# Two-layer graph network with a 4096 x 4096 adjacency matrix: high parts of split units copied into three matmul banks as well, low parts subtracted from there piece by piece

## What is computed

```python
def _lap_mul(A, x):
    d = 1.0 / jnp.sqrt(jnp.sum(A, axis=-1))
    return d[:, None] * (A @ (d[:, None] * x))
# layer 0, on h = relu(layernorm(x))
z = leaky_relu(_lap_mul(A, h) @ W1 + b1)                 # first product with A
d2 = max(|z_i|^2 + |z_j|^2 - 2 z_i.z_j, 0)               # distances of all pairs
S = exp(-sqrt(d2 + 1e-10) / 2), kept for the 4 best of each row, else 0
x = x + _lap_mul(S + A, h) @ W2 + b2                     # second product with A
# layer 1, on h = relu(layernorm(x))
x = x + h @ W_self.T + (A @ h) @ W_neigh.T + b           # third product with A
```

## Time and profile before

| | us |
|---|---|
| median of 3 runs | 1177.01 |
| lowest, highest run | 1172.3, 1194.65 |
| the profiled execution | 1180.82 |
| its span, first to last instruction | 1178.8 |
| TensorE busy (matmuls) | 929.5 (79%) |
| VectorE busy | 868.9 (74%) |
| GpSimd busy | 680.8 (58%) |
| ScalarE busy | 566.7 (48%) |

### The profile page before, as it was taken

One profiled execution on the slowest core, in us unless ns is written; L12 is line 12 of the kernel. 1 busy time (PEld: TensorE's weight loads), 2 busy tenths in 40 slices (PEclk: granted clock), 3 DMA queues, 4 the chain that ended last, 5 costly groups with the idle time before them and its releaser, 6 DMA issues.

```text
span 1178.8 us, 12596 instructions
## 1 busy us (share of the span) xinstructions
PE 929.5 (79%) x3378; PEld 583.5 (50%) x3378; DVE 868.9 (74%) x960; ACT 566.7 (48%) x1171; POOL 680.8 (58%) x1103
## 2 busy tenths in 40 slices
PE   0146437549559788769999999979989997999997
PEld 0023213224224333346766766435656645788886
DVE  2648558757768999747999998627687648888884
ACT  2454434545422221147777778424334433676763
POOL 9999988878673668104555565667777763000000
PEclk9987679689789888979999999999999998899999
DMA  9999999999999999739766767998989997699992
GB/s 210 293 315 321 330 331 363 341 335 359 361 333 358 339 313 356 296 125 367 260 250 247 256 235 270 395 412 316 349 299 356 371 341 269 248 369 383 376 387 90
DMA packets 98750, 369.10 MB, mean 313 GB/s; under 512 B 21264, under 2 KB 34320, under 8 KB 73872
## 3 DMA queue, kind: packets, MB, share of 16 engines
q1 hardware_dynamic: 51696, 258.43, 56.6%
q0 software_dynamic: 40960, 103.87, 30.7%
q10 hardware_dynamic: 6048, 6.29, 1.6%
HBM read 244.78 MB, written 123.73 MB: 313 GB/s over the span
## 4 chain that ended last, share of the span: by engine, by line
PE 41%; DVE 7%; POOL 5%; issue 4%; DMA 3%; ACT 2%; POOLq 0%; ACTq 0%; DVEq 0%
PE ps L1362 6%; PE ps L1380 5%; PE ps L1381 5%; PE ps L1382 5%; PE ps L1363 5%; PE ps L1364 5%; PE ps L1389 4%; POOL zt_lo L613 3%; PE ps L1359 2%; DVE araw_r L1207 2%; DVE araw L936 1%; DMA araw<-in_adj_dram 1%; DVE out_t L1164 1%; PE ps L1259 1%; PE ps L1271 1%
## 5 line engine op out<-in xcount | busy, mean ns | idle before, releaser
L389 POOL DMA_DIRECT2D araw<-in_adj_dram x704 | 382.7, 552 | 88.5 <-DVE tr L936 48.9
L1207 DVE TENSOR_TENSOR araw_r<-araw,tr_r 128x512 fp32r<-128x512 f32 (+1 forms) x184 | 213.9, 1220 | 63.4 <-ACT tr_r L815 63.3
L815 ACT ACTIVATE tr_r<-araw 128x2048 fp32r<-128x2048 f32 x88 | 166.3, 1910 | 74.4 <-DMA araw<-transposed 29.6
L613 POOL DMA_INDIRECT zt_lo<-neighbour_table,idx_st x128 | 144.2, 1126 | 48.8 <-issue 42.3
L761 ACT ACTIVATE araw<-ps,nsq 128x1024 f32<-128x1024 f32 x128 | 142.6, 1117 | 55.4 <-PE ps L1364 55.4
L1271 PE MATMUL ps<-tr,ys 128*128 128x512 f32 x256 | 130.7, 661 | 35.5 <-DVE ys L943 28.5
L659 ACT ACTIVATE ps<-araw 128x256 f32<-128x256 f32 x304 | 111.6, 367 | 81.9 <-DMA araw<-in_adj_dram 81.4
L936 DVE STREAM_TRANSPOSE tr<-araw 128x2048 f32<-128x2048 f32 x32 | 123.3, 3873 | 30.3 <-DMA araw<-in_adj_dram 26.7
L1389 PE MATMUL ps<-araw,ys 128*128 128x512 f32 x320 | 142.9, 602 | 2.6 <-ACT ys L806 2.6
L1362 PE MATMUL ps<-zt_lo,zs_hi 128*128 128x512 f32 x256 | 108.8, 425 | 0.0
L1066 DVE TENSOR_REDUCE bmax<-araw 128x64 f32<-128x4096 f32 x23 | 101.5, 4411 | 9.4 <-ACT araw L761 7.4
(11 more groups left out here) (164 smaller groups left out, 1460.7 us busy)
## 6 DMA issues: line engine op xcount, KB each, us to landing
araw<-transposed SPq DMA_DIRECT2D x128, 1024.0 KB, 7.1
araw<-in_adj_dram POOLq DMA_DIRECT2D x704, 128.0 KB, 16.2
keys_scratch<-araw SPq DMA_DIRECT2D x96, 512.0 KB, 3.5
transposed<-tr SPq DMA_DIRECT2D x32, 1024.0 KB, 8.6
transposed<-unit_zt_hi SPq DMA_DIRECT2D x8, 1024.0 KB, 9.3
transposed<-unit_zt_lo SPq DMA_DIRECT2D x8, 1024.0 KB, 8.7
transposed<-unit_sq_rows SPq DMA_DIRECT2D x8, 1024.0 KB, 9.5
transposed<-araw SPq DMA_DIRECT2D x8, 1024.0 KB, 5.3
```

Of the source, the lines that this page charges most:

```text
L389: gp.dma_start(araw[R * q:R * q + R, place, U * v:U * v + U], adj_v[q, :, g // 2, g % 2, v, :, c]).then_inc(a_first_in[place], DMA)
L613: gp.indirect_dma_start(out=gath[:, i, u, k, :], out_offset=None, in_=table, in_offset=bass.IndirectOffsetOnAxis(ap=idx_st[:, i, u * TOPK ...
L815: act.activation(ring_hi[:, place % TSLOTS], ring[:, j], ACT.Copy).then_inc(hi_done, 1)
L1207: ins = v.tensor_tensor(ring_lo[:, j, u], ring[:, j, u], ring_hi[:, place % TSLOTS, u].bitcast(F32), ALU.subtract)
```

## The change

In the second product (g2 < 8), ScalarE copies each 512-column piece of the high part once more, from SBUF into one of three PSUM banks (5, 6, 7 in turn), after it has waited for the end of its own 2048-column copy. A copy into a bank waits until VectorE has done the subtraction that read the bank last (`lo_piece`). VectorE's subtraction takes the high part from the bank (`hi_piece`) instead of from SBUF, and raises `lo_piece` per piece. TensorE waits for the count of pieces in the second product, and for `lo_done`, which now counts the third product's units alone, in the third.

```diff
--- before.py
+++ after.py
@@ -189,6 +189,7 @@
         ps_t = ps[:, 3]
         ps_q = ps[:, 4]
         ps_d = ps[:, 5]
+        hi_banks = [ps[:, 5 + i] for i in range(3)]
         junk = [ps[:, 6], ps[:, 7]]
 
         x_in = sem("x_in")
@@ -239,6 +240,8 @@
         h_hi_done = sem("h_hi_done")
         hi_done = sem("hi_done")
         lo_done = sem("lo_done")
+        hi_piece = sem("hi_piece")
+        lo_piece = sem("lo_piece")
         lane_max = sem("lane_max")
         lane_found = sem("lane_found")
         block_maxima = sem("block_maxima")
@@ -813,6 +816,13 @@
                     act.wait_ge(u_used, used_before(g2, j))
                 act.wait_ge(a_in[j], g2 * DMA + DMA)
                 act.activation(ring_hi[:, place % TSLOTS], ring[:, j], ACT.Copy).then_inc(hi_done, 1)
+                if g2 < GROUPS:
+                    act.wait_ge(hi_done, place + 1)
+                    for u in range(U):
+                        n = place * U + u
+                        if n >= len(hi_banks):
+                            act.wait_ge(lo_piece, n - len(hi_banks) + 1)
+                        act.activation(hi_banks[n % len(hi_banks)], ring_hi[:, place % TSLOTS, u].bitcast(F32), ACT.Copy).then_inc(hi_piece, 1)
 
             def evacuate(g, bank, used, turn):
 
@@ -1202,6 +1212,12 @@
             def split_low(g2, j):
 
                 place = split_place(g2, j)
+                if g2 < GROUPS:
+                    for u in range(U):
+                        n = place * U + u
+                        v.wait_ge(hi_piece, n + 1)
+                        v.tensor_tensor(ring_lo[:, j, u], ring[:, j, u], hi_banks[n % len(hi_banks)], ALU.subtract).then_inc(lo_piece, 1)
+                    return
                 v.wait_ge(hi_done, place + 1)
                 for u in range(U) if g2 <= GROUPS else (slice(0, U),):
                     ins = v.tensor_tensor(ring_lo[:, j, u], ring[:, j, u], ring_hi[:, place % TSLOTS, u].bitcast(F32), ALU.subtract)
@@ -1372,9 +1388,9 @@
                 for par in range(2):
                     distances(pair * 2 + par, par)
 
-            def unit(g2, j, bank, hi, lo, place, ready, first, last):
-
-                pe.wait_ge(lo_done, ready)
+            def unit(g2, j, bank, hi, lo, place, split_done, ready, first, last):
+
+                pe.wait_ge(split_done, ready)
                 for i in range(U):
                     t_hi, t_lo = ring_hi[:, place % TSLOTS, i], ring_lo[:, j, i]
                     pe.matmul(acc[bank], hi[:, i], t_lo, start=first and i == 0, stop=False)
@@ -1416,7 +1432,7 @@
                 else:
                     if isinstance(g, int) and g == 1:
                         pe.wait_ge(y_lo_done, j - WHOLE + 1)
-                    unit(g, j, i, y_split[:, j], y_split[:, j - WHOLE], j - WHOLE, g * TSLOTS + (j - GROUPS + 1), False, j == GROUPS - 1)
+                    unit(g, j, i, y_split[:, j], y_split[:, j - WHOLE], j - WHOLE, lo_piece, g * (TSLOTS * U) + (j - GROUPS + 1) * U, False, j == GROUPS - 1)
 
             def group_second(g, i, turn=1):
                 pe.wait_ge(acc_read, g + (2 * GROUPS - 3))
@@ -1437,7 +1453,7 @@
             def group_third(g, i, prev):
                 pe.wait_ge(acc_read, g + (3 * GROUPS - 3))
                 for j in range(GROUPS):
-                    unit(g + GROUPS, j, i, hi_g[:, j], lo_g[:, j], j, g * GROUPS + ((GROUPS - 2) * TSLOTS + j + 1), j == 0, j == GROUPS - 1)
+                    unit(g + GROUPS, j, i, hi_g[:, j], lo_g[:, j], j, lo_done, g * GROUPS + (j + 1), j == 0, j == GROUPS - 1)
                     if prev is not None and j == 0:
                         finish_third(prev)
 
@@ -1470,7 +1486,7 @@
             pe.wait_ge(acc_read, 3 * GROUPS - 3)
             for j in range(GROUPS):
                 pe.wait_ge(kept, j + 2)
-                unit(GROUPS, j, 0, hi_g[:, j], lo_g[:, j], j, (GROUPS - 2) * TSLOTS + j + 1, j == 0, j == GROUPS - 1)
+                unit(GROUPS, j, 0, hi_g[:, j], lo_g[:, j], j, lo_done, j + 1, j == 0, j == GROUPS - 1)
                 if j == 0:
                     finish_second_b(GROUPS - 2)
                     finish_second_a(GROUPS - 1)
```

## The result

The changed kernel took 1206.3 us (median of five runs, 1204.9 to 1230.0), the kernel before 1177.0 (five runs, 1172.3 to 1194.7). The ratio is 1.033 with a 95% interval of 1.026 to 1.040: slower by over 2%, and outside the range of 1173 to 1201. The profiled execution took 1206.0, its span is 1204.1. Medians and ranges in this text take in all runs; a ratio, with its 95% interval in brackets, takes only runs within 1.5% of the kernel's fastest and compares them with such runs of the kernel before in the same set.

The account below looks back on a forecast made before the run. TensorE was taken to bound the kernel; ScalarE's lengthened loop makes it 11.5 us late in the second product, reduced to 5.8 + 1.7 = 7.5 at the third's start: 1177.0 + 7.5 = 1184.5, said as 1185, range 1173 to 1201.

Parts of the forecast that it names:

- Waits: Second product: behind ScalarE's copies stand the evacuation (reading a finished group from its bank), c's input and the next unit.
- c's input: ScalarE's copy feeding TensorE's finishing step c, after the evacuation; with the evacuation counted as 2 x 0.48 us per group.
- the loop's 4.5 us of slack: ScalarE and VectorE's loop took 21.97 us per group against TensorE's 26.44, leaving 4.5 us to spare.
- Prices: Copy 587 ns, 0.50 us each in a run; unit 3.94 us on ScalarE, was 1.80; subtraction 0.61 to 0.69 us.
- Rival 1: Copies cost more, unpipelined 0.65 us, a unit 4.54: 1196 us, or 1202 with slower subtractions; chance 0.18.
- The loop: Second product, ScalarE and VectorE per group: 27.9 us, 1.5 above TensorE's 26.44; evacuation over 12.4 us after the loop's start.
- N(3): ScalarE's start on the next group's split units after normalizing, for group 3: forecast at 842.9 us, was 841.41.
- a(5): TensorE's finishing step a of group 5, waiting for the evacuation: forecast at 939.0 us, was 927.54, so 11.5 late.
- GpSimd freed: Gathers take 1.50 us beside two-SBUF-input subtractions, 1.01 alone; PSUM input may end them microseconds sooner, counted 0 for that alone.
- rival 2: Not slower: copies hide in the loop's slack and freed GpSimd removes a 7.7 us block: 1172 us; chance 0.14.
- The start of the third product: Sums of group 7 begin 5.8 us late, plus 1.7 for VectorE standing still beside GpSimd's adds: 7.5 us.
- Rival 3: VectorE's standing still at the third product's start stays whole: +11.5 us, 1188.5; sign a VectorE piece over 7 us; chance 0.14.

Follow-up runs that it names:

- changed, 2nd profile: The changed kernel run again with no edit, on the first chip: 1193.5 us against 1180.0, ratio 1.013.
- copies only: The changed kernel, but VectorE takes the high part from SBUF while ScalarE still copies into the banks: 1195.5 us, ratio 1.016.
- bank reads only: The changed kernel without ScalarE's copies; VectorE subtracts whatever lies in the banks, so low parts are meaningless: 1175.2 us, ratio 0.987.
- changed, 3rd profile: The changed kernel run once more with no edit, on the second chip: 1216.3 us against 1181.6, ratio 1.039.
- before, again: The kernel before run again with no edit, on the second chip: 1192.5 us against 1183.8 for the same code, ratio 1.013.
- no gathers after group 1: The changed kernel without the gathers of groups 2 to 7, so their output is wrong: 1189.3 us, ratio 1.013.
- plain rows: The changed kernel with each gather by index replaced by a GpSimd-issued plain transfer of as many rows from fixed places: 1194.1 us, ratio 1.011.
- moved adds: GpSimd's bias add of group g put after the first eight gathers of group g+3, in the kernel before (first ratio 1.003) and in the changed one.

## Why the prediction missed

The profiles side by side, clean ones first (rest: from the high copy of (1,6) to the end, us; late: of all updates, and after that copy; the chip of the first comparison is not known):

```
kernel                   chip   span    rest    late        late in the rest
before                    -     1178.8  385.7     1/2041      1/504
changed, 2nd profile      1st   1190.4  398.8     2/2209      1/658
copies only               1st   1189.2  400.0     0/2209      0/658
bank reads only           1st   1177.6  376.3     0/2113      0/570
changed, 1st profile      -     1204.1  419.5   288/2209    155/658
changed, 3rd profile      2nd   1219.9  423.4   317/2209    158/658
before, again             2nd   1195.4  398.3   238/2041     99/504
no gathers after group 1  2nd   1184.9  396.7   182/2209     33/658
plain rows                3rd   1190.8  393.9   157/2209      0/653
```

The step that failed stands under "Waits" and in the sum. The prediction saw that c's input stands behind ScalarE's copies, gave it 0.48 us per group and no wait, and counted the loss of the loop's 4.5 us of slack as 1.5 us per group and nothing else. In the measured execution c's input stood for 14.72 and 2.77 us, 17.5 in all, for semaphore updates that came late. Nothing in the trace of before showed such waits.

- **The rest was forecast as 385.7 + 7.5 = 393.2. It is 398.8 where next to no update is late, and 419.5 in the measured execution.** So 5.6 us are an error of the sum, and 20.7 a cost that the sum did not have.
- **Prices (right, unit 0.08 too small).** Copy 587 ns, unit 4.02 (3.94), subtraction 682, no fight over the banks, ScalarE busy 617.8 us instead of 566.7 (some 56 more predicted, 51.1 found, since copies in a run overlap). Rival 1 is out: high copies are 4.02 apart, not 4.5.
- **The loop (right, slightly small).** 28.4 us per group instead of 27.9: the 0.08 per unit, and 0.2 for the sums. N(3) comes 1.1 later than worked out from the high copy of (1,6), and the evacuation is over at N + 12.7 instead of 12.4. So in the clean profile a(5) starts 148.9 us after that copy, where 146.0 was forecast: **2.9 of the 5.6**.
- **GpSimd freed (right).** 1022 ns per gather instead of 1126, and none over 1.15 us, where the kernel before has 24 over 1.3, up to 1.50. Rows 8 and the rule of the Trainium skill (SBUF — State Buffer, Who interferes with whom) were borne out. (For an instruction with one SBUF input that section of the Trainium skill states the rule only outside VectorE's 2-port modes, which the prediction left out.) Bank reads only shows that rival 2's mechanism is real and larger than I had it (9.4, not 5), but only with high parts that cost ScalarE nothing.
- **The start of the third product (mis-sized).** The step was "I take 1.7 for it", which left a relief of 4.0. In the clean profile a(5) is 14.4 late and the end 13.1: a relief of 1.3, **2.7 of the 5.6**. I had looked for the adds in the 24 pieces only. They now fall on VectorE's small steps and sums before these pieces, which also stand before the sums of group 7: in the clean profile one of 4 columns (L1194, 0.17 to 0.22 us in the measured execution) took 5.93 us while five adds ran, and ended with them. It has one SBUF input, so the rule as the prediction gives it would have left it free.

```profile
974.93 5.93 DVE L1194 TENSOR_SCALAR tmp<-mv 128x4 f32<-128x4 f32 x1
```

```profile
974.67 6.15 POOL L642 TENSOR_TENSOR xs<-xs,bias 128x512 f32<-128x512 f32 x5
```

- Moving the adds took 4.6 us off that stretch of the changed kernel, where the sum had allowed 1.7 for them: 2.9 too little, about the 2.7 that is missing. Rival 3 ("the still stand stays whole"), given 0.14, was nearer than the forecast here, though not by its sign: no piece of VectorE was long.
- **What the sum did not have.** Late updates, 20.7 us (24.6 in the third profile); 17.5 of them are the two waits of c's input. Behind the same high copy TensorE stands for 48.1 us instead of 34.0 in the clean profile, 14.1 more; the other 6.7 are longer matmuls, at a mean granted clock of 0.93 instead of 0.95.
- **Why they are dearer now.** The kernel before has late updates too, for 12.6 us in one profile and, with moved adds, for 0.9 and 1.5. Its loop had 4.5 us to spare per group and covered a late 3.47 us whole. The changed kernel has nothing to spare: from group 3 to group 4 its loop takes 43.3 us (835.59 to 878.84) instead of 28.4, that is the 14.72 in full. So much is shown. That the slack makes the whole difference is argued: the waits themselves were longer in the changed kernel, and no run isolates the two.
- **Luck.** Only the profiled execution of before is known to have had no late updates in the first comparison; whether its other runs had them is not known, and the 3.3% may contain that luck.
- **The forecast for the time.** Where updates were not late the changed kernel took 1193.5, inside the range; its ratio of 1.013 is no more than two series of one kernel differ by, and it is the rest, 13.1 us longer, that shows the loss. In the first comparison it was 3.3%, on the second chip 3.9%. The chance of 0.10 for slower by over 2% rested on the price of a copy alone. It should have held a case "ScalarE's loop has no slack left, so anything unforeseen is paid in full".

## What to carry to other kernels

Work put on an engine whose loop is close to the period of the bound engine costs twice: what sticks out of the period (here 2 us per group), and the slack that had covered disturbances nobody had counted. Freeing another engine is worth something only where it is waited for: reading from the banks was worth 9.4 us without the copies and 1.2 with them. And GpSimd instructions that aren't urgent (here the adds) belong where VectorE is idle, not in a row where it starts a new stage.

## What the runs showed of the hardware that was not expected

- On two of three chips about a tenth of all semaphore updates (224 to 317 of some 2100, in kernels with all their gathers) have no record near the end of their instruction, from the first gather by index (about 520 us) until shortly after the last; on one chip 0 to 2 in four kernels. Some of them took effect in time, others late; the one followed closest was 22.7 us late. While no gather by index ran there were none (plain rows, no gathers), and with pauses after every four few (29 instead of about 155). The mechanism is not shown, nor is whether it also happens in an execution that nobody traces.
- It cost between 0.9 and 24.6 us per execution here, and the count doesn't tell which: 224 late updates cost 0.9, 238 cost 12.6, 288 cost 20.7.
- In such a stretch engines issue slowly too: two single transposes of 0.37 us in the changed kernel start 1.40 us apart (850.25 and 851.65 above), each after more than 1 us of "issue". The profile names such a wait "remote" or "issue", never its cause.
- A ScalarE copy of 512 columns into PSUM takes 587 ns and comes every 0.52 us in a run; one into SBUF takes 631 ns.
- Five adds of GpSimd in a row (6.15 us) held a VectorE instruction of 4 columns for 5.93 us: it went on only when the last of them was over.
- GpSimd needs 1.02 us to issue a gather of 128 rows by index and 0.54 for a plain transfer of as many.
